# A two-task mixture of experts on one core: the last dot product of each task on VectorE and one matmul with ones

## The reference

```
h = relu(x @ eW1 + eb1); h = relu(h @ eW2 + eb2); expert_out = h @ eW3 + eb3      (8 experts)
gates = softmax(x @ gW + gb)                                                      (2 tasks x 8 experts)
tin = sum over experts of gates * expert_out                                      (2 tasks, 256 wide)
th = relu(tin @ tW1 + tb1)        256 to 512
th = relu(th @ tW2 + tb2)         512 to 256
out = sigmoid(th @ tW3 + tb3)     256 to 1        -> out[512, 2]
```

## Time and profile before

| | |
|---|---|
| median of 3 runs | 611.92 us (611.56 to 612.14) |
| span of the profiled execution, first to last instruction | 609.9 us |
| its own time beside the span: the median less the span | 2.0 us around it |
| TensorE matmul busy | 605.4 us (99%), 2,657 matmuls |
| TensorE weight load busy | 499.1 us (82%) |
| VectorE busy | 279.4 us (46%) |
| ScalarE busy | 189.1 us (31%) |
| GpSimd busy | 38.9 us (6%) |
| mean granted TensorE clock | 0.996 of full speed |

### The profile page before, as it was taken

One profiled execution on the slowest core, in us unless ns is written; L12 is line 12 of the kernel. 1 busy time (PEld: TensorE's weight loads), 2 busy tenths in 40 slices (PEclk: granted clock), 3 DMA queues, 4 the chain that ended last, 5 costly groups with the idle time before them and its releaser, 6 DMA issues.

```text
span 609.9 us, 7183 instructions
## 1 busy us (share of the span) xinstructions
PE 605.4 (99%) x2657; PEld 499.1 (82%) x2657; DVE 279.4 (46%) x389; ACT 189.1 (31%) x224; POOL 38.9 (6%) x37
## 2 busy tenths in 40 slices
PE   9999999999999999999999999999999999999998
PEld 6888888888888888888888888888888888888787
DVE  7625336345256345254354353463352552553770
ACT  3422325313233223233133232232332242332351
POOL 1000000030001100030000300020000300003000
PEclk9999999999999999999999999999999999999998
DMA  8830097206231172204421073201623054310000
GB/s 312 319 103 1 3 369 287 69 0 219 93 101 34 29 244 71 103 0 147 161 75 63 0 237 102 82 26 59 217 69 103 0 173 137 103 34 0 1 1 0
DMA packets 33577, 63.25 MB, mean 104 GB/s; under 512 B 2064, under 2 KB 7312, under 8 KB 33440
## 3 DMA queue, kind: packets, MB, share of 16 engines
q1 hardware_dynamic: 33248, 58.64, 28.6%
q0 software_dynamic: 176, 4.23, 1.8%
q10 hardware_dynamic: 144, 0.26, 0.1%
HBM read 63.08 MB, written 0.04 MB: 103 GB/s over the span
## 4 chain that ended last, share of the span: by engine, by line
PE 99%; DVE 1%; ACT 0%; issue 0%; DVEq 0%; ACTq 0%
PE bank L194 32%; PE bank L195 32%; PE bank L196 32%; PE bank L417 1%; PE bank L371 1%; PE bank L288 1%; PE bank L348 0%; PE bank L347 0%; DVE w_lo L526 0%; ACT w_hi L436 0%; DVE h_lo L539 0%; PE bank L365 0%; PE bank L357 0%; DVE h_hi L537 0%; DVE warm L587 0%
## 5 line engine op out<-in xcount | busy, mean ns | idle before, releaser
L526 DVE TENSOR_TENSOR w_lo<-w_raw,w_hi 128x1024 fp32r<-128x1024 f32 x99 | 121.0, 1224 | 239.0 <-ACT w_hi L436 238.8
L194 PE MATMUL bank<-x_hi,w_hi 128*128 128x512 f32 x524 | 204.1, 389 | 0.4 <-issue 0.4
L196 PE MATMUL bank<-x_hi,w_lo 128*128 128x512 f32 x524 | 203.9, 389 | 0.0
L195 PE MATMUL bank<-x_lo,w_hi 128*128 128x512 f32 x524 | 203.9, 389 | 0.0
L436 ACT ACTIVATE w_hi<-w_raw 128x1024 fp32r<-128x1024 f32 x99 | 104.8, 1059 | 282.9 <-PE bank L196 263.8
L194 PE MATMUL bank<-h_hi,w_hi 128*128 128x512 f32 x336 | 131.1, 390 | 0.1
L195 PE MATMUL bank<-h_lo,w_hi 128*128 128x512 f32 x336 | 130.8, 389 | 0.0
L196 PE MATMUL bank<-h_hi,w_lo 128*128 128x512 f32 x336 | 130.7, 389 | 0.0
L194 PEld LDWEIGHTS bank<-x_hi,w_hi 128*128 128x128 f32 x524 | 98.3, 188 | 21.6 <-issue 0.8
L196 PEld LDWEIGHTS bank<-x_hi,w_lo 128*128 128x128 f32 x524 | 98.4, 188 | 20.4
L195 PEld LDWEIGHTS bank<-x_lo,w_hi 128*128 128x128 f32 x524 | 98.4, 188 | 20.2
(11 more groups left out here) (59 smaller groups left out, 80.9 us busy)
## 6 DMA issues: line engine op xcount, KB each, us to landing
w_raw<-eW SPq DMA_DIRECT2D x103, 512.0 KB, 4.0
gates_all<-gates_dram POOLq DMA_DIRECT2D x1, 4096.0 KB, 14.0
w_raw<-tW SPq DMA_DIRECT2D x4, 512.0 KB, 3.5
gates_all<-xT SPq DMA_DIRECT2D x7, 256.0 KB, 6.4
w_raw<-eW SPq DMA_DIRECT2D x2, 256.0 KB, 4.1
gates_all<-xT ACTq DMA_DIRECT2D x1, 256.0 KB, 3.9
prm<-small SPq DMA_DIRECT2D x1, 164.0 KB, 8.4
gates_dram<-turned POOLq DMA_DIRECT2D x1, 32.0 KB, 2.0
```

Source lines behind the costliest of these rows:

```text
L194: pe.matmul(bank[:], weights_hi, moving_hi, start=first, stop=False)
L195: pe.matmul(bank[:], weights_hi, moving_lo, start=False, stop=False)
L196: return pe.matmul(bank[:], weights_lo, moving_hi, start=False, stop=last)
L526: dve.tensor_tensor(w_lo[:, j % RING, :], raw_piece(j), w_hi[:, j % RING, :].bitcast(F32), ALU.subtract).then_inc(w_ready, 1)
```

## The change

The last dot product is done in another way. VectorE multiplies tile 0 of a task with its column of `tW3`, one weight per partition, and then adds tile 1 times its own column: 128 partitions x 512 rows are left for each task. One matmul for each task, with a column of ones as stationary side and these 512 columns as moving side, in plain f32, sums over the partitions into one row of 512. ScalarE squashes that row with Sigmoid and the bias `tb3` and writes it into partition 0 of `task_in` with the two tasks interleaved. SyncE stores the 4 KB of that one partition. Sigmoid is first called on a dummy, behind the last split of weights and ahead of the copies of line 505. VectorE sets the ones at the start.

```diff
-BANK_FINAL = 6
+BANK_FINAL = [6, 7]
...
-        fin = sb("fin", [4, BT * T])
+        ones = sb("ones", [1])
+        squash_sink = sb("squash_sink", [1])
+        result = task_in[:, 0:T, :].rearrange("p t b -> p (t b)").rearrange("p (b t) -> p b t", t=T)
...
-            sp.wait_ge(fin_step, 4)
-            sp.dma_start(out.rearrange("(p b) t -> p (b t)", p=P), fin[:, 3, :]).then_inc(out_stored, DMA)
+            sp.wait_ge(squashed, T)
+            sp.dma_start(out.rearrange("(o b) t -> o (b t)", o=1),
+                         result[0:1].rearrange("o b t -> o (b t)")).then_inc(out_stored, DMA)
...
-            for n, (t, k) in enumerate([(t, k) for t in range(T) for k in range(KT1)]):
-                pe.wait_ge(tower2_ready, n + 1)
-                for b in range(BT):
-                    mm = pe.matmul(banks[BANK_FINAL][:, b * T + t:b * T + t + 1],
-                                   gated[:, n, :].rearrange("p (q b) -> p q b", b=BT)[:, :, b],
-                                   prm_of("tw3", n), start=(n == 0 and b == 0), stop=(n == T * KT1 - 1 and b == BT - 1),
-                                   skip_group_check=True)
-            mm.then_inc(final_done, 1)
+            for t in range(T):
+                if t == 0:
+                    pe.wait_ge(ones_ready, 1)
+                pe.wait_ge(folded, t + 1)
+                pe.matmul(banks[BANK_FINAL[t]][0:1, :], ones[:], gated[:, t * KT1, :],
+                          start=True, stop=True).then_inc(final_done, 1)
...
+            act.wait_ge(ones_ready, 1)
+            act.activation(squash_sink[:], ones[:], ACT.Sigmoid).then_inc(squash_warm, 1)
...
-            act.wait_ge(fin_step, 1)
-            act.activation(fin[:, 1, :], fin[:, 0, :], ACT.Exp, scale=-1.0).then_inc(fin_exp, 1)
+            for t in range(T):
+                act.wait_ge(final_done, t + 1)
+                act.activation(result[0:1, :, t], banks[BANK_FINAL[t]][0:1, :], ACT.Sigmoid,
+                               bias=prm_of("tb3", t)[0:1, :]).then_inc(squashed, 1)
...
+            dve.memset(ones[:], 1.0).then_inc(ones_ready, 1)
...
-            dve.wait_ge(final_done, 1)
-            dve.tensor_tensor(fin[:, 0, :], banks[BANK_FINAL][:, 0:BT * T], prm_of("tb3", 0, BT * T),
-                              ALU.add).then_inc(fin_step, 1)
-            dve.wait_ge(fin_exp, 1)
-            dve.tensor_scalar(fin[:, 2, :], fin[:, 1, :], 1.0, None, ALU.add).then_inc(fin_step, 2)
-            dve.wait_ge(fin_step, 3)
-            dve.reciprocal(fin[:, 3, :], fin[:, 2, :]).then_inc(fin_step, 1)
+            for t in range(T):
+                dve.wait_ge(tower2_ready, t * KT1 + 1)
+                dve.tensor_scalar(gated[:, t * KT1, :], gated[:, t * KT1, :], prm_of("tw3", t * KT1), None,
+                                  ALU.mult).then_inc(weighed, 1)
+                dve.wait_ge(tower2_ready, t * KT1 + 2)
+                dve.wait_ge(weighed, t + 1)
+                dve.scalar_tensor_tensor(gated[:, t * KT1, :], gated[:, t * KT1 + 1, :], prm_of("tw3", t * KT1 + 1),
+                                         gated[:, t * KT1, :], ALU.mult, ALU.add).then_inc(folded, 1)
```

More of the change, by code:

```diff
@@ L162, in moe_towers @@
         final_done = sem("final_done")
-        fin_step = sem("fin_step")
-        fin_exp = sem("fin_exp")
+        ones_ready = sem("ones_ready")
+        squash_warm = sem("squash_warm")
+        weighed = sem("weighed")
+        folded = sem("folded")
+        squashed = sem("squashed")
         out_stored = sem("out_stored")
```

## The result

The changed kernel takes 606.67 us (median of 4 runs, 606.44 to 606.77), the kernel before 611.78 us (4 runs, 611.56 to 612.14; the 611.92 above is the median of the first three): 5.1 us less, a ratio of 0.9914 (95% interval 0.9902 to 0.9926). Forecast were 607.1 us, in a range of 606.2 to 608.5, and a gain of 4.8.

The account below looks back on a forecast made before the run. TensorE's matmul stream was taken to bound the kernel, with 10.0 us behind its last wide matmul. 8.19 us go and 3.38 come, a gain of 4.8: 611.92 - 4.8 = 607.1 us, range 606.2 to 608.5.

Parts of the forecast that it names:

- line 417 and the four small steps gone: After the last wide matmul: 7.23 us of small matmuls and 0.96 of bias, Exp, plus one, reciprocal go, 8.19 us.
- Relu exposed, with its release: Last Relu of line 516 on ScalarE, task 1, tile 1, stays in place and is now exposed: 0.72 us.
- fold, with its release: VectorE's scalar_tensor_tensor over 128x512 behind the last Relu, all operands in SBUF: 0.70 us, 0.73 with release.
- sum, with release and weight load: TensorE's plain f32 matmul with ones behind the fold: four passes 1.07 us, plus 0.14 ahead, 1.21.
- Sigmoid, with its release: ScalarE squashes 512 columns out of PSUM behind the second sum: 0.69 us, 0.72 with release.
- store to the end of the span: 4 KB store from one partition, last Sigmoid to span's end: kept at 1.86 us, 0.08 less allowed.
- sum behind the tower: All steps from the last wide matmul's end at 599.90 to the span's end, forecast at 605.14: 5.24 us.
- around the span: Time outside the profiled span, 609.9 against a median of 611.92: 2.0 us, taken to stay.
- Rival B: Sigmoid's table load on ScalarE not covered, or more than one needed: 1.28 us on the path, 608.4 us; chance 0.05.
- Rival A: TensorE's final sums slow, at half clock or 0.42 us passes: 1.0 us later, 608.1 us; chance 0.09.
- Rival C: Final store cut into 1,024 packets of 4 bytes on one queue: 8.6 us later, 615.7 us; chance 0.03.
- Rival D: Removed work at the end returns as small unpriced waits (semaphores, issue): within noise, 611.5 to 612.5 us; chance 0.04.

## Why the prediction was right

Taken by its own steps, each against the changed kernel's trace:

| step | forecast us | measured us |
|---|---|---|
| line 417 and the four small steps gone | 8.19 | 8.19 before, none after |
| Relu exposed, with its release | 0.72 | 0.72 |
| fold, with its release | 0.73 | 0.78 |
| sum, with release and weight load | 1.21 | 1.08 |
| Sigmoid, with its release | 0.72 | 0.73 |
| store to the end of the span | 1.86 | 1.67 |
| sum behind the tower | 5.24 | 4.98 |
| around the span | 2.0 | 1.8 |

The mechanism was right: what stood behind the last tower matmul was a chain without overlap, and it was exchanged for a shorter one. That line 417's time is that of its weight loads is borne out twice: half the blocks take half the time (3.60), and with one column of weights and 2,048 moving columns in all, where line 417 has 16, the four sums of the run without the fold take 3.54.

The gain of 4.8 was low by 0.26 on the path, for three mis-sized terms, one of which went the other way. (1) The sum: the release and the weight load of 0.14 stood ahead of it in the forecast. In the trace the matmul record starts with its weight load (601.56), 0.05 behind the fold, and four passes are 1.02 and not 1.07, as they follow each other at 0.21 and not at the 0.227 of the weight-load-and-matmul pairs of the towers. (2) The store: one packet lands 0.19 earlier than 144, which I had bounded at 0.08. I also read its parts wrongly, though not their sum: the 1.4 of the earlier trace rows counts from the start of the issue, so it holds the 0.36, and the last 0.4 us of the span lie behind the landing, before and after alike. SyncE waits for the landing 1.1 us behind its issue before and 0.9 after. (3) The fold was 0.05 dearer: with all operands in SBUF it takes 750 ns, as the form with a PSUM operand of the earlier trace rows, and not the 688 of the tensor_tensor. I had chosen by the memory; here the operation counted.

A rival that the prediction does not name: the clock fell to half in the middle of line 417, so a part of its 7.25 us could be the fallen clock's. The trace rules it out. Six matmul records that reach into 603 to 604 (clock 1.00) and six into 605 to 606 (0.50) take the same 1.54 us. That is 0.233 us from start to start and 0.37 for the last one; the 0.227 of the prediction is 7.25 by 32, and the first two records start only 0.03 apart. The two lines:

```profile
602.79 1.54 PE L417 MATMUL bank<-prm,gated 128*128 128x1 f32 x6
...
604.66 1.54 PE L417 MATMUL bank<-prm,gated 128*128 128x1 f32 x6
```

The time of 607.1 has further errors, and they partly hide one another. I took the 2.0 us around the span from a profiled execution and a median that don't belong together. In the runs with both numbers the time is 1.73 to 1.85 above the span, before and after alike. Nothing lies there that the change touched. From 607.12 go 0.26 on the path and 0.20 around the span, and 0.11 come for the tower's later end: 606.77, the time of the profiled run. The median of the four runs lies 0.10 below it. How near the time came is in part luck; that the steps came within 0.26 is not.

Costed at nothing and rightly so: the table load and the dummy (1.28 and 0.20 in the gap of 3.09, with 1.57 left), the memset of the ones, the scaling (0.49, done 1.5 us before the last Relu starts), the first sum and Sigmoid. Rival B (an uncovered load) did not come about. It gave one load on the path 1.28 us, and beside it said that one behind the last Relu would only push the first Sigmoid. The run without the dummy bears out the second: it costs 0.01.

Rival A (slow sum) did not come about: the clock stood at 1.00 to 604, and the sum was over at 602.58. Rival C (store by words) did not come about for this kernel, which stores one packet. As a mechanism it is real and I priced it at less than half: 19.3 us in place of 8.6. The price of a packet was right for the most part; the pauses and the late completion were not in it. Rival D (the removed work comes back in small waits) did not come about: the releases between the steps are 0.02 to 0.05 us each, near the 0.03 to 0.04 costed.

## What to carry to other kernels

A dot product at the end of a matmul-bound kernel should not load its activations as weights for one moving column: each 128x128 block in plain f32 cost 0.45 us here for a single column. Make the short side stationary and let the 512 columns move, fold on an idle engine what can be folded before, and put the results so that the store is contiguous, if need be by a strided write of the engine (0.02 us) and not by the DMA (19.3 us). Where the end is a chain of full-width steps on different engines, cutting the last tile into halves gains without any step becoming faster: here as much (0.63 us) as the f32r sum, which shortens one step by 0.63 and rounds the folded values. The gain ends where one engine is busy throughout.

## What the runs showed of the hardware that was not expected

A store of 1,024 words of 4 bytes from one partition to DRAM takes 21.0 us to the end of the span, 40 ns of engine time a packet in the mean and 9 in the median; the same 4 KB as one packet takes 1.67 us in all, and as 128 pieces of 32 bytes 1.86. A table load on ScalarE starts as soon as the engine is free, ahead of the wait that the activation behind it has, and nothing but its 1.28 us is seen. A plain f32 matmul with 512 moving columns is two records, 1.02 us alone and 0.86 in a row, where f32r takes 0.39 alone. Products of 128x128 plain f32 weights with one moving column followed each other 0.233 us apart (records), at a granted clock of 1.00 and of 0.50 alike.
